# First expansion: all rows of dst lanes as bytes in two loads each, row stores in three pieces

## The reference, cut to what matters

```python
def _L0_gnn_ref(x, edge_index, W1, b1, W2, b2):
    src, dst = (edge_index[0], edge_index[1])
    xs, xd = (x[src], x[dst])
    ...
    F_s = householder(reflection(xs, xd))
    F_d = householder(reflection(xd, xs))
    ...
    out = x - jnp.zeros_like(x).at[src].add(msg_s) - jnp.zeros_like(x).at[dst].add(msg_d)
    return jax.nn.relu(out)
def _L1_gnn_ref(x, edge_index, W1, b1, W2, b2):
    ...
    h = jnp.tanh(gcn_conv(x, W1, b1))
    h = jnp.tanh(gcn_conv(h, W2, b2))
    return h
x = _layernorm(x + _L0_gnn_ref(x, edge_index, ...), axis=-1)
x = _layernorm(x + _L1_gnn_ref(x, edge_index, ...), axis=-1)
```

## Time and profile before

| what | us |
|---|---|
| median of 3 runs | 7359.98 |
| lowest and highest run | 7352.93, 7368.35 |
| span of the profiled execution | 7361.5 |
| busy in the span: DVE | 6335.9 |
| busy in the span: ACT | 4842.1 |
| busy in the span: PE | 4369.6 |
| busy in the span: POOL | 2840.7 |
| first comparison of the expansion starts | 1401.9 |
| first instruction of DVE after the expansion's last waits | 2347.95 |

### The profile page before, as it was taken

How to read it: one execution, slowest core, us unless ns; L and a number is a source line. 1 busy time by engine, 2 the same in 40 slices (tenths; PEclk the granted TensorE clock), 3 DMA queues, 4 the chain that set the end, 5 groups by cost and what they waited for, 6 DMA issues and landing times.

```text
span 7361.5 us, 242681 instructions
## 1 busy us (share of the span) xinstructions
PE 4369.6 (59%) x83922; PEld 3504.3 (48%) x83922; DVE 6335.9 (86%) x9628; ACT 4842.1 (66%) x13310; POOL 2840.7 (39%) x2217
## 2 busy tenths in 40 slices
PE   1442000376665888888888888766566655566554
PEld 0342000266664555555555555555456544565443
DVE  4679997344445899999999999999999999999999
ACT  1665104122222899999999999899666677566776
POOL 5222304566764222222222222278500388200686
PEclk6666555688887898999889998887765699666898
DMA  4100000488876333333333333244499644799444
GB/s 63 8 8 8 4 0 26 148 297 298 299 288 218 120 117 118 116 118 116 116 116 116 117 117 117 88 121 120 105 294 291 211 120 120 200 293 295 127 121 95
DMA packets 510685, 1043.90 MB, mean 142 GB/s; under 512 B 125636, under 2 KB 316452, under 8 KB 497540
## 3 DMA queue, kind: packets, MB, share of 16 engines
q1 hardware_dynamic: 376804, 761.05, 30.1%
q0 software_dynamic: 113920, 281.72, 15.9%
q10 hardware_dynamic: 19872, 0.11, 0.2%
HBM read 756.44 MB, written 286.18 MB: 142 GB/s over the span
## 4 chain that ended last, share of the span: by engine, by line
DVE 28%; issue 27%; PE 12%; ACT 10%; POOL 10%; DVEq 5%; ACTq 3%; another core or an unknown queue 2%; DMA 1%; SPq 0%; POOLq 0%
PE ps L1118 7%; POOL got L638 4%; POOL sw_inb L638 4%; DVE xs_ring L1864 4%; PE ps L1259 3%; DVE wide_hotb L1987 3%; DVE keys L1476 3%; DVEq L1758 3%; ACT apartb L959 2%; DVE lane_hot L1754 2%; ACT step_lo L738 2%; DVE prods L1832 2%; ACTq L1006 2%; DVE keys L1475 2%
## 5 line engine op out<-in xcount | busy, mean ns | idle before, releaser
L638 POOL DMA_INDIRECT xs_ring<-xd_rows,src_idx x488 | 595.3, 1220 | 1803.8 <-DVE xs_ring L1864 1663.8
L1987 DVE TENSOR_SCALAR wide_hotb<-sw_inb,slot_id 128x2048 bf16<-128x2048 bf16 x976 | 923.2, 1014 | 57.5 <-PE ps L1259 57.3
L1754 DVE TENSOR_TENSOR wide_hotb<-dst_key,iota_b 128x1792 bf16<-128x1792 bf16 x879 | 949.0, 1080 | 8.5 <-ACT val_out L1017 4.4
L1259 PE MATMUL ps<-wide_tabb,wide_hotb 128*128 128x48 bf16 x15616 | 640.1, 207 | 360.9 <-DVE wide_hotb L1987 232.3
L638 POOL DMA_INDIRECT got<-val_rows,dst_idx x296 | 396.7, 1340 | 1177.3 <-DMA val_rows<-val_out 1085.9
L1118 PE MATMUL ps<-row_tab,dst_hot 128*128 128x64 bf16 x15744 | 656.0, 203 | 295.7 <-issue 244.9
L1259 PEld LDWEIGHTS ps<-wide_tabb,wide_hotb 128*128 128x128 bf16 x15616 | 592.0, 112 | 409.2 <-ACT val_out L1017 315.2
L1148 PEld LDWEIGHTS ps<-wide_tab,wide_hot 128*128 128x128 bf16 x23424 | 617.8, 99 | 347.8 <-DVE wide_hot L1748 309.1
L1118 PEld LDWEIGHTS ps<-row_tab,dst_hot 128*128 128x128 bf16 x15744 | 577.1, 104 | 374.9 <-issue 340.0
L638 POOL DMA_INDIRECT src_key<-chunk_keys,src_idx x488 | 622.0, 1275 | 335.5 <-ACT xd_out L801 187.3
L1148 PE MATMUL ps<-wide_tab,wide_hot 128*128 128x32 bf16 x23424 | 642.4, 181 | 89.0 <-DVE wide_hot L1748 84.0
(11 more groups left out here) (416 smaller groups left out, 11818.9 us busy)
## 6 DMA issues: line engine op xcount, KB each, us to landing
dw_in<-dst_wide SPq DMA_DIRECT2D x96, 1312.0 KB
xd_rows<-xd_out SPq DMA_DIRECT2D x128, 984.0 KB
sw_in<-src_wide SPq DMA_DIRECT2D x244, 512.0 KB
sw_inb<-src_wide SPq DMA_DIRECT2D x244, 512.0 KB, 5.1
val_rows<-val_out SPq DMA_DIRECT2D x488, 192.0 KB, 4.1
sw_inb<-src_byte SPq DMA_DIRECT2D x244, 256.0 KB, 4.4
msg_rows<-msg_out SPq DMA_DIRECT2D x244, 200.0 KB, 2.8
dw_in<-dst_byte SPq DMA_DIRECT2D x32, 656.0 KB
```

Source lines behind the costliest of these rows:

```text
L638: return pool.indirect_dma_start(out=into, out_offset=None, in_=table, in_offset=bass.IndirectOffsetOnAxis(index, 0))
L1259: last = mm(ps_val[s * 2 + h][:, t, :], wide_hot2[s][:, half, e:e + P], wide_tab2[s][:, h, half * 3 * D:(half + 1) * 3 * D], start=half == ...
L1754: return v.tensor_tensor(to.rearrange("p t (j k) -> p t j k", k=2), rel.unsqueeze(2).to_broadcast(shape), iota_b[:, 0:w].rearrange("p (j k ...
L1987: last = v.tensor_scalar(wide_hot2[q % 2][:, half, :], sw_in2[q][:, :], slot_id[:, half:half + 1], None, ALU.is_equal)
```

## The change

All four kinds of row load bytes from `dst_byte`, so all four `dw_in` are byte tiles, and DVE compares bytes in all 128 rows. A row's load is two transfers of 2624 places. A row's store is three transfers, one for each unit, each after the wait for its own unit; `xd_stored` so rises by 48 a row, and all that wait for it or for `wide_got` count accordingly. `dst_wide` is still written.

```diff
-        dw_in = [sb(f"dw_in{k}", [P, WID], U8 if k == 3 else BF16, of=pc) for k in range(4)]
+        dw_in = [sb(f"dw_in{k}", [P, WID], U8, of=pc) for k in range(4)]
...
+        ROW_LOADS = 2
+        LOADED = WID // ROW_LOADS
+        WIDE_GOT = 16 * ROW_LOADS * (P // 4)
...
             def load_wide(i, k):
-                rows = dst_byte_v if k == 3 else dst_wide_v
-                sp.dma_start(dw_in[k][:, :], rows[bass.ds((i * 4 + k) * WID, WID)].partition_broadcast(P)).then_inc(wide_got[k], 16)
+                rows = dst_byte_v
+                for c in range(ROW_LOADS):
+                    sp.dma_start(dw_in[k][:, c * LOADED:(c + 1) * LOADED],
+                                 rows[bass.ds((i * 4 + k) * WID + c * LOADED, LOADED)].partition_broadcast(P)).then_inc(wide_got[k], 16)
 
             def store_row(i, k):
-                sp.wait_ge(unit_chosen, i * 12 + (3 * k + 3))
-                sp.dma_start(xd_v[:, bass.ds(i * 4 + k, 1), :],
-                             xd_out[k][:, :, :].rearrange("p t c -> p (t c)").unsqueeze(1)).then_inc(xd_stored[k], 16)
+                for n, (c, d) in enumerate(UNITS):
+                    sp.wait_ge(unit_chosen, i * 12 + (3 * k + n + 1))
+                    sp.dma_start(xd_v[:, bass.ds(i * 4 + k, 1), c * XW:d * XW],
+                                 xd_out[k][:, c:d, :].rearrange("p t c -> p (t c)").unsqueeze(1)).then_inc(xd_stored[k], 16)
...
-                        act.wait_ge(xd_stored[k], i * 16)
+                        act.wait_ge(xd_stored[k], i * 48)
...
-                dve.wait_ge(wide_got[k], i * 16 + 16)
+                dve.wait_ge(wide_got[k], i * (16 * ROW_LOADS) + 16 * ROW_LOADS)
```

More of the change, by code:

```diff
@@ L680, in _ @@
             for k in range(4):
-                pool.wait_ge(xd_stored[k], 16 * (P // 4))
+                pool.wait_ge(xd_stored[k], 48 * (P // 4))
             pool.wait_ge(wide_stored, 32)
@@ L1714, in _ @@
             for k in range(4):
-                dve.wait_ge(xd_stored[k], 16 * (P // 4))
+                dve.wait_ge(xd_stored[k], 48 * (P // 4))
             dve.wait_ge(keys_got, 16 * NST)
@@ L1982, in expand_hots @@
                     loads = (G + 7 - q) // 8
-                    dve.wait_ge(wide_got[q], i * 16 + ((P // 4 if q < 4 else 0) * 16 + (l - 1) * 16 * loads + 16))
+                    dve.wait_ge(wide_got[q], i * 16 + ((WIDE_GOT if q < 4 else 0) + (l - 1) * 16 * loads + 16))
                     if warm:
```

## The result

The changed kernel takes 7407.87 us (median, 7402.71 to 7416.23) against 7356.45 for the kernel before in the same runs: a ratio of 1.007, 95% interval 1.0056 to 1.0085. It is slower by 51 us, where 23 us less were forecast.

The account below looks back on a forecast made before the run. It took TensorE's supply, likely slowed by transfers, to bound the rows; with quicker rows the gathers end the stage: 1416.3 + 607.3 + 300 = 2323.6, 23 us earlier, so 7337 us, range 7308 to 7366.

Parts of the forecast that it names:

- What bounds the kernel now: First expansion: no engine full, waits decide; TensorE's supply slows rows to 7.35 us, transfers the likely reason.
- Part 1, 5.7 us a row: Row loop: byte loads shrink four rows from 8528 to 6560 KB, so a row takes 5.7 us instead of 7.35.
- Rival 1: Row loop: rows do not get quicker, TensorE's gaps are not from the bytes; 7360 us, chance 0.12.
- it is hidden as long as a row takes over about 4.8 us: VectorE: 96 longer comparisons add 131 us, hidden behind the row; without cover up to 175 us.
- Part 2: SP's two loads and three stores a row: 1.75 us of issuing, hidden; no packet overhead taken for shorter pieces.
- Rival 4: Row transfers: each piece pays its own latency, 11.3 us a row, 7865 us; a quarter uncovered 7373; chance 0.07.
- Where the gain goes: POOL's gathers fall behind the quicker rows and set the stage's end, 23 us earlier than now.
- One of the prediction's own signs: Profile after: gathers wait for ScalarE only at their start, are busy 760 us; still waiting inside the stage refutes it.
- 2.4 forecast: POOL's gathers: each of 125 comparisons holds them 2.4 us, 300 us in all; ends 2.2 and 2.6.
- The sum by its own terms: Last gather's end: start 1416.3, plus 607.3 for 488 gathers, plus 300 of holds, gives 2323.6 us.
- Rival 2: POOL's gathers are held less by comparisons, 250 us in all; 7287 us, chance 0.06.
- rival 3: Stage's end: gathers don't set it, the rows' end at 2135 decides; about 7150 us, chance 0.03.

Follow-up runs that it names:

- x_nodma_2: Kernel before with no row loads in the loop and its stores moved behind the loop, run again: 7627.46 us against 7346.56.
- x_twice: Kernel before with each bf16 comparison done twice, first into a spare tile: 7089.85 us against 7015.86, ratio 1.0099.
- f_bytes_ahead: Kernel before with bytes in all rows, four dst_hot buffers and the comparison one row ahead; one load, one store: 7151.14 us, ratio 1.0186.
- f_after_ahead: Changed kernel with dst_hot in four buffers and the comparison one row ahead of the choosing: 7130.85 us against 7016.57, ratio 1.016.
- f_before_ahead: Kernel before, its row types kept, with four dst_hot buffers and the comparison one row ahead: 7007.33 us, ratio 0.9982.
- f_wide_ahead: Kernel before with bf16 in all rows, four dst_hot buffers and the comparison one row ahead: 6978.31 us, ratio 0.9936; again 6982.5, 0.9952.
- after_again: Changed kernel, unchanged, run again against the kernel before: 7396.79 us against 7346.56, ratio 1.0064.
- v_allwide: Kernel before with bf16 for all rows, one load and one store each: 7328.12 us, ratio 0.9982.
- x_lategather: Kernel before with POOL's gathers let go only after the last row's copies: 7521.98 us against 7013.3.
- x_alone: Kernel before with no loads, no stores and no gathers while the rows run: 7368.79 us against 7013.3.
- v_bytes: Kernel before with bytes for all rows, one load and one store a row as before: 7396.22 us against 7358.4, ratio 1.0046.
- v_2loads: Kernel before with each row's load in two pieces, types as before: 7355.39 us, ratio 0.999.

## Why the prediction was wrong

**What bounds the kernel now.** "The row loop is thus slowed in TensorE's supply" was right. "The transfers are the likely reason" was wrong at the level that was forecast, and it is the step that failed. I took bytes over rate (29.6 us for four rows) as support because it met the row time; any kernel in a steady state moves its bytes at bytes over time, so the agreement said nothing. The row of 7.35 us with 2 GB/s in `x_nodma_2` is the test that this ratio is not. At level 7010 the transfers do set the rows (5.69 us with the types of before in the order one row ahead, 4.20 without the loads in the old order; with bytes it is 4.46, and VectorE is busy all the time), but no row there was at hand for the prediction.

**Part 1, 5.7 us a row.** The term was 7.35 - 5.7 = 1.65 us a row gained; it measured -0.29 with bytes alone and -0.39 with the whole change. Rival 1 had the first half of this (rows no quicker, 0.12), but not the loss. For a slower kernel I had 0.11 in all.

**Part 1, "it is hidden as long as a row takes over about 4.8 us".** Wrong at level 7350: the rows took 7.35 us, VectorE was half idle, and the change of type in 96 rows still cost 38 us, some 0.4 us each. (The bound that the prediction gives for no cover, 1.36 us x 128 = 175 us, should have 96 in place of 128, as its +131 us has.) My reading is that a mean hides the cost. TensorE works in bursts of 33 ns a matmul, 4.1 us a row, and then pauses. Within a burst VectorE's 4.6 us of choosing and comparing are as long as the row, so there is no slack exactly where TensorE could be quick. In the trace the cost shows as longer pauses (0.19 us a row) and slower matmuls with more time at the lower clock (0.32), not as waits for dst_hot (26.8 us after against 25.6 before). The link from the longer comparison to these is argued and not shown, and so is that it is the length: `x_twice`, `f_bytes_ahead` and `f_after_ahead` were made to test it and all met level 7010. So why bytes cost 38 us at level 7350 stays open.

**Part 2.** That pieces cost nothing was right for the types of before (0.9996 and 0.999). Beside bytes two loads cost some 15 us by one series. Rival 4 is out in its full form, as a row with five transfers takes 4.79 us at level 7010; its mild form, a quarter uncovered, had 7.45 us a row and 7373 us. The section of the Trainium skill named beside it is on transfers issued by GpSimd, as its title says, and SP issues these; no run measured one of them alone.

**Where the gain goes.** The mechanism, that long comparisons hold the gathers and the gathers then set the end, was right, and it did not decide at level 7350, where the rows are late themselves. One of the prediction's own signs told so: the gathers should have waited for ScalarE at their start alone (48.7 us), and waited 111.8. The held time there is 743.0 - 459 = 284 us, 2.22 a comparison against 2.4 forecast. At level 7010 it decides: 2.47 us a comparison in `f_bytes_ahead`, and rows that end 371 us ahead of the gathers. The sum by its own terms (1205.8 + 607.3 + 316 = 2129) misses the 2143.5 of `f_bytes_ahead` by 14 us, of which 10 are longer pauses between gathers ("issue" 159.4 us in all against 487 x 0.305 = 149) and 3 waits for the first rows' copies. Rival 2 is out by these rows. Of rival 3 the name came true, as the rows' end decided, but not its reason, rows that end early. The whole change in the order of before was not run at level 7010, so its own cost there is open; with the order one row ahead it is 1.6%.

**The expectations of the runs.** For level 7010 I expected rows of the types before at 5.7 us, set by transfers, with the gathers last: `f_before_ahead` has 5.69, and there the gathers do end last. `f_bytes_ahead` and its two companions had expectations for level 7350 alone, which stay unanswered; that the supply of instructions sets a row, as both expectations of `f_wide_ahead` say, no run shows. `f_after_ahead` came out below its 7145 to 7160, since its gathers are busy for 752.6 us, so a comparison holds them 2.30 us and not 2.45. `after_again` showed a row of 7.84, 0.1 more than the first time, so a row at level 7350 is known to about 0.1 us.

The best version of the study is `f_wide_ahead`: bf16 in all rows, one load, one store, four dst_hot buffers. It beats the kernel before in two series at level 7010 (0.9936 and 0.9952), where the changed kernel was run with that order alone (1.016). It was not run at level 7350, where bf16 in all rows with the old order is 0.9982.

## What to carry to other kernels

Bytes over rate meets the row time of every steady loop, so it can't show that transfers set it: take the transfers out in one run before pricing a smaller load. An engine that is half idle on average may have no slack in the bursts of the engine that it feeds, so price a longer step on it from zero to its whole length. And before a variant is priced on a term, see whether the kernel before itself runs at one level: here two levels 345 us apart made another chain decide. An indirect transfer issued by GpSimd is held by every long VectorE comparison that it meets, so a cheaper load that is paid with a longer comparison is paid a second time there.

## What the runs showed of the hardware that was not expected

- The same kernel took 7070.64 us at one time and 7627.46 at another, with rows of 4.19 and 7.35 us. In the rows the difference is in pauses of 0.3 to 1.5 us between matmuls without any wait, four a row, which come at some times and not at others. At level 7350 they are there with 2 GB/s of transfers (`x_nodma_2`) and with 324 (`v_allwide`), and at level 7010 they are all but gone even with 393 (`x_lategather`). VectorE shows such pauses too, and behind the stage the two executions differ by 9 us only.
- A gather that is running when a comparison starts ends 0.12 us after it; one that starts inside it ends 0.81 to 0.83 us after it. In 128 long comparisons that made 2.22 to 2.47 us each. With no comparison beside them (`x_alone`) none of the 488 gathers took over 0.99 us.
- From SP's issue to a load's first packet, by the packets' start times, whole rows of bf16 took 2.0 us and whole rows of bytes 1.0 (kernel before, `v_bytes`); of two half rows of bytes the first took 1.0 and the second 2.3 to 2.4 (changed kernel). So the 1.0 for the kernel before in the expectation of `v_2loads` holds for its byte rows alone. At level 7350 no wait of VectorE for a load came of it.
